# A vision tower on one Trainium2 core: the row norm, the rank sums and two loads of the last stage, written another way

## Time and profile before

| | us |
|---|---|
| median of 3 runs (lowest to highest) | 3320.6 (3319.63 to 3323.88) |
| the profiled execution, own time | 3318.28 |
| its span, first to last instruction | 3316.4 |
| mean granted TensorE clock, share of full speed | 0.901 |

### The profile page before, as it was taken

One profiled execution on the slowest core, in us unless ns is written; L12 is line 12 of the kernel. 1 busy time (PEld: TensorE's weight loads), 2 busy tenths in 40 slices (PEclk: granted clock), 3 DMA queues, 4 the chain that ended last, 5 costly groups with the idle time before them and its releaser, 6 DMA issues.

```text
span 3316.4 us, 69976 instructions
## 1 busy us (share of the span) xinstructions
PE 2775.0 (84%) x25687; PEld 2181.5 (66%) x25687; DVE 1901.2 (57%) x4527; ACT 1843.2 (56%) x3725; POOL 1134.6 (34%) x964
## 2 busy tenths in 40 slices
PE   6999999999999859999996677877788777877787
PEld 4766666666666549999995456655566555655565
DVE  4878878878788742222221355655565555655566
ACT  4777777777777734444443345544454444544454
POOL 1454555655555530000002533333333333333310
PEclk9999999999999979999998688887888888878888
DMA  3222222222222137777774111111111111111110
GB/s 119 88 84 72 96 83 72 101 78 75 100 76 73 42 114 228 228 230 227 230 228 140 34 40 41 29 41 44 44 40 27 43 44 43 40 28 44 44 30 26
DMA packets 139758, 287.14 MB, mean 87 GB/s; under 512 B 25440, under 2 KB 82784, under 8 KB 135392
## 3 DMA queue, kind: packets, MB, share of 16 engines
q1 hardware_dynamic: 114912, 245.68, 22.9%
q0 software_dynamic: 24576, 37.80, 4.2%
HBM read 215.08 MB, written 68.29 MB: 85 GB/s over the span
## 4 chain that ended last, share of the span: by engine, by line
PE 47%; issue 7%; another core or an unknown queue 4%; DVE 3%; ACT 1%; POOL 1%; DMA 0%; SPq 0%; DVEq 0%; ACTq 0%; POOLq 0%
PE psum L1174 8%; PE psum L1165 8%; PE psum L1538 7%; PE psum L1498 5%; PE psum L1555 3%; PE psum L1568 3%; PE psum L1523 2%; PE psum L1503 2%; PE psum L1580 2%; DVE qdiag L1837 1%; PE psum L1598 1%; PE psum L1156 1%; PE psum L1546 1%; DVE inv L1852 1%
## 5 line engine op out<-in xcount | busy, mean ns | idle before, releaser
L1466 POOL DMA_INDIRECT ycho<-expert_out,place x384 | 367.5, 957 | 1417.4 <-DVE place L1829 1309.7
L1208 ACT ACTIVATE hid<-psum,w_blk 128x256 f32<-128x256 f32 x608 | 269.1, 474 | 326.2 <-PE psum L1165 326.2
L1039 POOL DMA_INDIRECT expert_in<-rows,slot_i x384 | 392.3, 1022 | 133.2 <-issue 111.6
L1852 DVE RECIPROCAL inv<-psum 128x64 f32<-128x64 f32 x288 | 159.5, 554 | 464.7 <-remote 385.9
L1538 PE MATMUL psum<-keys,qdiag 64*64 64x80 f32 x4608 | 281.4, 256 | 124.1 <-issue 123.7
L1752 ACT ACTIVATE ex<-psum,smin 128x80 f32<-128x80 f32 x1152 | 282.2, 332 | 142.9 <-DVE smin L1845 135.8
L1538 PEld LDWEIGHTS psum<-keys,qdiag 64*64 64x64 f32 x4608 | 214.8, 148 | 211.1 <-issue 195.7
L502 PE MATMUL psum<-xn,w_in 128*128 128x288 f32 x1024 | 311.1, 429 | 39.6 <-DVE xn L861 10.2
L1174 PE MATMUL psum<-w_blk,hid 128*128 128x128 f32 x2432 | 296.6, 275 | 0.0
L1568 PE MATMUL psum<-ex_t,pair_ones 128*32 128x64 f32 x4608 | 137.8, 244 | 189.6 <-DVE half L1853 124.0
L1165 PE MATMUL psum<-x_t,w_blk 128*128 128x256 f32 x1216 | 289.5, 381 | 2.4 <-DMA w_blk<-w_exp_in 2.4
(11 more groups left out here) (247 smaller groups left out, 5848.5 us busy)
## 6 DMA issues: line engine op xcount, KB each, us to landing
w_blk<-w_exp_in SPq DMA_DIRECT2D x152, 578.0 KB, 3.8
xin<-x_in SPq DMA_DIRECT2D x32, 1716.0 KB
rows_in<-expert_in SPq DMA_DIRECT2D x152, 128.0 KB, 2.3
expert_out<-rows_out SPq DMA_DIRECT2D x152, 128.0 KB, 3.0
h_dram<-h SPq DMA_DIRECT2D x32, 288.0 KB
x_dram<-x SPq DMA_DIRECT2D x32, 288.0 KB
h1c<-h_dram SPq DMA_DIRECT2D x32, 288.0 KB
x2c<-x_dram SPq DMA_DIRECT2D x32, 288.0 KB
```

The source lines that it names most:

```text
L1039: pool.indirect_dma_start(out=expert_in[:, :], out_offset=bass.IndirectOffsetOnAxis(ap=slot_i[z.s][:, n:n + 1], axis=0), in_=rows[z.s][:, ...
L1208: nc.scalar.activation(hid[b.s][:, c, :], HB[b.s][c % HK], ACT.Gelu_apprx_tanh, bias=w_blk[b.q][:, FF + FC * D + c:FF + FC * D + c + 1]).t ...
L1466: pool.indirect_dma_start(out=ycho[x.s][:, k, :], out_offset=None, in_=expert_out[:, :], in_offset=bass.IndirectOffsetOnAxis(ap=place[x.s] ...
L1852: v.reciprocal(inv[:], sum_bank()).then_inc(head_step, 1)
```

## The change

In words, by stage:

- **First stage.** `picks` lies by expert and then group, and a scan on VectorE makes `upto_g`, its running sum over the groups, in place of the reduction to `newly`. With `before` now 1 less everywhere (so -1 or 0), three products give the ranks: `before` with `picks`, ones with `upto_g`, ones with `chosen`. They wait for step 15 of the router instead of 13. One ACT table load per step is dropped. x2 is stored as rows from `rows`, not as columns from `x2`.
- **Constants.** `shift3` is center times ln3_b, and `att_bias` takes ln3_b up.
- **Third stage.** x2c is loaded as rows. POOL adds it to the first half of the products (a second add), then the second half, to `ysum`. Norm3 works on the rows: `row_halves` (six bn_stats) and `row_stats` (six bn_aggr) on VectorE, `row_root` (Ln, Exp on 96x6) on ScalarE, `row_moves` (-mean times root) on VectorE, and `normed_rows`, six Identity passes with scale and bias per token, on ScalarE. `moe` turns the normed rows into A1 where the centring stood, and VectorE makes h2 from it in one instruction. `prec`, x3, the square, the two products and the root of norm3 are gone, as is the old `moe` at the end of a step. The square of norm4 and `xq` add shift3.
- **Loads.** `load(v, x)`: x2c waits until scores of unit 4 of item x are done, h1c until those of unit 6; before, both were issued without such a wait. The gathers and the load of x2c wait for `ysum`'s step of two items before.

The diff, cut to its core:

```diff
-        "before": (p[:, None] < p[None, :])[:, :G],
+        "before": (p[:, None] < p[None, :])[:, :G] - 1.0,
...
                 if z:
-                    hold(sp, x2_step, z.upto(2, 2))
-                    sp.dma_start(x2_dram[:, a_range(z.n, z.s)], x2[z.s][:]).then_inc(x2_stored[z.s], 16)
+                    hold(sp, rows_ready, z.upto(2, 2))
+                    sp.dma_start(x2_dram[row_range(z.n, z.s), :], rows[z.s][:].rearrange("p g d -> p (g d)")
+                                 ).then_inc(x2_stored[z.s], 16)
...
-                pe.wait_ge(route_step, z.upto(ROUTE, 13))
+                pe.wait_ge(route_step, z.upto(ROUTE, 15))
...
-                nc.tensor.matmul(dst, C("before")[0:G, :], picks[z.s][:], start=True, stop=False)
-                for g in range(NG - 1):
-                    nc.tensor.matmul(dst[:, g + 1:NG, :], C("ones")[0:G, 0:G],
-                                     picks[z.s][:, g:g + 1, :].to_broadcast([G, NG - 1 - g, E]),
-                                     start=False, stop=False)
+                nc.tensor.matmul(dst, C("before")[0:G, :], by_group(picks[z.s][:]), start=True, stop=False)
+                nc.tensor.matmul(dst, C("ones")[0:G, 0:G], by_group(upto_g[z.s][:]), start=False, stop=False)
...
-                act.preload_act_table_set("gelu_apprx_tanh_and_others")
...
-            v.tensor_reduce(newly[s][:], picks[s][:].rearrange("p g e -> p e g"), AX_X, ALU.add
-                            ).then_inc(route_step, 1)
+            v.tensor_tensor_scan(upto_g[s][:], within[:], picks[s][:], 0.0, ALU.mult, ALU.add).then_inc(route_step, 1)
...
-            def load(x):
+            def load(x, during):
+                if during:
+                    hold(sp, scores_done, during.upto(NU, 4))
+                if x.old(2):
+                    hold(sp, ysum_step, x.upto(YSUM, -YSUM))
+                sp.dma_start(x2c[x.s][:].rearrange("p g d -> p (g d)"), x2_dram[row_range(x.n, x.s), :]
+                             ).then_inc(x2_landed[x.s], 16)
+                if during:
+                    hold(sp, scores_done, during.upto(NU, 6))
                 if x.old(2):
                     hold(sp, h2_ready, x.upto(1, -1))
                 sp.dma_start(h1c[x.s][:], h1_dram[:, a_range(x.n, x.s)]).then_inc(h_landed[x.s], 16)
-                sp.dma_start(x2c[x.s][:], x2_dram[:, a_range(x.n, x.s)]).then_inc(h_landed[x.s], 16)
...
-                pool.wait_ge(ysum_step, x.upto(2, 1))
+                pool.wait_ge(x2_landed[x.s], 16 * x.n + 16)
+                pool.wait_ge(ysum_step, x.upto(YSUM, 1))
+                pool.tensor_tensor(x2c[x.s][:], x2c[x.s][:], ycho[x.s][:, 0:NG, :], ALU.add).then_inc(ysum_step, 1)
+                pool.wait_ge(ysum_step, x.upto(YSUM, 2))
                 if x.old(1):
-                    pool.wait_ge(moe_done, x.upto(1, 0))
-                pool.tensor_tensor(ysum[:], ycho[x.s][:, 0:NG, :], ycho[x.s][:, NG:, :], ALU.add
-                                   ).then_inc(ysum_step, 1)
+                    pool.wait_ge(nrows_ready, x.upto(1, 0))
+                pool.tensor_tensor(ysum[:], x2c[x.s][:], ycho[x.s][:, NG:, :], ALU.add).then_inc(ysum_step, 1)
...
-                    pe.wait_ge(prec_ready, w.upto(1, 1))
-                    project(A1, C("center"), prec[:]).then_inc(norm3_pe, 1)
+                    moe(w, A1)
...
+            def row_root(x):
+                act.wait_ge(stats_ready, x.upto(1, 1))
+                nc.scalar.activation(root3[:], stats[:, :, 1], ACT.Ln, bias=eps_col[0:G, 0:1]).then_inc(root_step, 1)
+                act.wait_ge(root_step, x.upto(2, 1))
+                nc.scalar.activation(root3[:], root3[:], ACT.Exp, scale=-0.5).then_inc(root_step, 1)
+
+            def normed_rows(x):
+                act.wait_ge(moved_ready, x.upto(1, 1))
+                if x.old(1):
+                    act.wait_ge(moe_done, x.upto(1, 0))
+                for g in range(NG):
+                    last = nc.scalar.activation(nrows[:, g, :], ysum[:, g, :], ACT.Identity, bias=move3[:, g:g + 1],
+                                                scale=root3[:, g:g + 1])
+                last.then_inc(nrows_ready, 1)
...
+            def row_halves(x):
+
+                v.wait_ge(ysum_step, x.upto(YSUM, YSUM))
+                for g in range(NG):
+                    last = v.bn_stats(halves3[:, g, :], ysum[:, g, :])
+                last.then_inc(halves3_ready, 1)
...
-                    v.scalar_tensor_tensor(out=two(x3[:]), in0=both(A1), scalar=V("ln3_g"), in1=two(r3[:]),
-                                           op0=ALU.mult, op1=ALU.mult).then_inc(x3_ready, 1)
+                    v.wait_ge(moe_done, w.upto(1, 1))
+                    v.wait_ge(h_landed[w.s], 16 * w.n + 16)
+                    v.scalar_tensor_tensor(out=two(h2[:, w.s * T:(w.s + 1) * T]), in0=both(A1), scalar=V("ln3_g"),
+                                           in1=two(h1c[w.s][:]), op0=ALU.mult, op1=ALU.add).then_inc(h2_ready, 1)
```

124 lines of the change are left out of this document (67 added, 57 removed).

## The result

The changed kernel takes **3355.7 us** (median of 4 runs, 3351.5 to 3359.0), the kernel before 3321.3 us in runs beside it: ratio **1.0106**, 95% interval 1.0094 to 1.0118, so 34.5 us slower. 3341 us was forecast, in the direction and within the range of the likeliest case (3328 to 3365). Its size fell short by 15 us. That the sum came out as near as this is in part luck: the errors of its terms nearly cancel, and one term is missing, as the last sections show.

What follows compares the result with a forecast made beforehand. Third-stage steps (45.7 us) were taken as bound by a gather stall, then a chain through ScalarE, VectorE and TensorE. 3318.3 + 29 - 8 - 2 + 1 = 3338.3, plus 2.3: 3341 us; 8-in-10 range 3250 to 3380.

Steps and rivals of the forecast that it cites:

- the likeliest case: Whole kernel: the forecast of 3341 us with its own range, 3328 to 3365 us, chance 0.44.
- The chain: Third stage: passes delay r5, xm, transposes, VectorE, ex and next xq; 1.0 us per step, +29 us in 29 steps.
- I take 0.28: Third stage, ScalarE: each of six Identity passes takes 0.28 us, 1.7 us together, ahead of the root r5.
- The meetings: Third stage: VectorE's att slowed by POOL's adds, 0.3 us at unit 2 and 0.35 at the att behind it.
- The loads: Third stage: two loads moved from beside the gathers to mid-step save 0.3 us in 28 steps, -8 us.
- TensorE bounds the step: Third-stage rival: 2.0 us less TensorE work shortens 31 steps, -62, so 3258 us, half 3289; chance 0.18, wholly or by half.
- First stage: First stage: fewer rank products free 0.7 us or so of TensorE, mostly taken back as waiting; -2 us.
- Its own sign: Third stage: if the forecast is right, mid-stage steps last 46.4 to 47 us instead of 45.7.
- The loads as the cause of the stall: Third-stage rival: loads, not gathers, idle the engines; moving them gives 6.2 us in 28 steps, about 3175 us; chance 0.10.
- fill and rest: Third stage's pipeline fill: a second add exposed in its first item, +1.8, less the loads' overlap, +1 us.

Runs made afterwards that it cites:

- experiment 1: The changed kernel with ScalarE's six passes on the rows moved behind the root r5 instead of ahead of it: 3337.7 us, ratio 0.999 to the kernel before.
- experiment 6: The changed kernel with the six passes behind the root r5 and both loads at the start of a step: 3352.8 us, ratio 1.0104 to the kernel before.
- experiment 2: The changed kernel with both loads issued at the start of a step again, without waits for scores: 3334.9 us, ratio 0.9984 to the kernel before.
- experiment 4: The kernel before with only its third-stage loads moved to mid-step, behind scores 4 and 6: 3343.0 us, ratio 1.0004 to the kernel before.
- experiment 7: The changed kernel with one gather per item instead of twelve, the rest zeros: 2913.3 us, ratio 0.8774 to the full kernel before.
- experiment 8: The kernel before with one gather per item instead of twelve, the rest zeros: 2923.0 us, ratio 0.8803 to the full kernel before.
- experiment 12: The changed kernel with the row norm moved into the gathers' idle time, h2 and its centring earlier, loads at step start: 3268.1 us, ratio 0.9845 to before.

## Why the prediction was right, and where it was not

- *The chain.* Its links were right: passes, r5, `xm`, transposes, VectorE, `ex`, `xq`. The terms were not. "I take 0.28" was the mis-sized one: a pass costs 0.40 (2.42 us for six), so r5 starts 2.3 us late instead of 1.5. The sum of 1.0 us per step came out at 0.8, at equal clock on A and without gathers on C; what took up the difference no run shows. Nor was r5 the one place that mattered: in experiments 1 and 6 it goes ahead of the passes, and TensorE stands still for nearly as long.
- *The meetings.* 0.3 and 0.35 us were taken, 0.35 and 0.27 us are the means over 25 steps; in the step shown the first is the full 1.6 us. In the length of a step both together are worth some 0.3 us by experiment 2, and that is an estimate across two chips.
- *The loads.* -8 us was wrong, experiment 4 gives 0. The stretch of the stall did get 0.3 us shorter on A and 0.1 us on B, but the end of the step did not come earlier.
- *TensorE bounds the step.* The forecast spoke against it with VectorE's wait of 1.14 us in the earlier trace rows. But that is a wait of VectorE for TensorE, and TensorE has no gap in before's busy part (0.02 us per step). So TensorE did bound it, on chip D over the whole step. What the rival had wrong is its condition: the passes do not finish in time. The work saved (1.5 us per step in experiments 7 and 8) is less than the waits that came in (2.3 us), and this difference is what the kernel lost at equal clock.
- *First stage.* -2 us was forecast. The result's own trace has -5.8 for the first two stages, the other chips -0.4 to -5.1. With the old first stage every third step on chip A takes 35.4 to 35.8 us instead of 35.0, in the changed kernel none more than 35.4; what lengthened them the rows don't say.
- *What was missing.* The steps' share in the clock's classes. The forecast treated the clock as given, and took 45.7 us for the length of a step, which is that of before's shortest class; the mean is 46.3. Its own sign, steps of 46.4 to 47 us, holds for 12 of the 28 steps, and the mean is 47.7. The later clock cost 16 to 19 us, nearly half of what the full steps lost, and it is why the total was 15 us low. What decides in which class a step falls stays open: chip B had nearly all steps of before's third stage in the last one.
- The loads as the cause of the stall fall by experiments 4 and 8. For that rival the Trainium skill ("Runtime: NRT & Kernel Launch", section "Instruction fetch mechanics") was cited; no run shows its blocks of instructions standing behind a load.

The forecast's terms beside those of the trace: chain +29, measured +22 at equal clock; loads -8, measured 0; first two stages -2, measured -6; fill and rest +1, measured +1; the clock 0, measured +16. The errors of the first three nearly cancel, and the missing one is what remains.

## What to carry to other kernels

Work taken off the engine that bounds a stage is worth only what is left after the waits that its replacement brings in: here 1.5 us of work against 2.3 us of waits. Before replacing it by work on another engine, look for the place in that engine's order where it idles anyway, as experiment 12 does, and count what stands queued behind the new instructions. Where the time depends on the clock or on the chip, compare steps of like clock, and kernels on one chip only.

## What the runs showed of the hardware that was not expected

- Chips differ by 15% in this kernel (2837.8 to 3341.8 us): in the traces from A, B, C and E, engines stand still while twelve indirect DMAs of 0.92 us each are issued, in those from D they run on.
- TensorE's granted clock fell a second time, within the busy part, where waits had come in: in 26 of 28 steps of experiment 6, at 35 us after the first gather, for 3.4 us.
- An Identity pass of 96x128 with a scale and a bias column takes 0.50 us, 0.38 from start to start; a bn_stats of 96x128 0.26 us, six of them 1.24 us.
